# Gated window attention with a routed second stage on one core: each 1024 KB output store issued as four stores of one chunk

## The reference

```python
def xattn(x, cond):                       # 8 heads of 32 channels, a window of 16 columns
    q, k, v = pointwise(Wq, bq, x), pointwise(Wk, bk, cond), pointwise(Wv, bv, cond)
    k_win, v_win = windows(k), windows(v)
    attn = softmax(einsum('bhdt,bhdtw->bhtw', q, k_win) * 32 ** -0.5)
    return pointwise(Wo, bo, einsum('bhtw,bhdtw->bhdt', attn, v_win))

def ffn(h):                               # 64 experts, the top 8; a row is 2048 columns of one channel
    scores = softmax(h @ router_weight.T + router_bias)
    w_dense = the 8 largest of scores, zero elsewhere
    return h * w_dense.sum(-1) + w_dense @ expert_bias

x = x + tanh(g_xattn) * xattn(layernorm(x), ctx)
x = x + tanh(g_ffn) * ffn(layernorm(x))
```

## Time and profile before

| | |
|---|---|
| median of three runs | 1551.26 us (1549.26 to 1552.44) |
| the profiled execution: its own time | 1557.26 us |
| its span | 1555.1 us |
| busy, share of the span | TensorE 94%, VectorE 82%, ScalarE 74%, GpSimd 74% |
| mean granted TensorE clock | 0.972 of full |
| DMA | 365577 packets, 210.39 MB, mean 135 GB/s |
| written to HBM | 33.55 MB, in 32 stores |

### The profile page before, as it was taken

One profiled execution on the slowest core, in us unless ns is written; L12 is line 12 of the kernel. 1 busy time (PEld: TensorE's weight loads), 2 busy tenths in 40 slices (PEclk: granted clock), 3 DMA queues, 4 the chain that ended last, 5 costly groups with the idle time before them and its releaser, 6 DMA issues.

```text
span 1555.1 us, 66658 instructions
## 1 busy us (share of the span) xinstructions
PE 1464.6 (94%) x28162; PEld 1199.9 (77%) x28162; DVE 1276.5 (82%) x2970; ACT 1144.8 (74%) x2009; POOL 1148.0 (74%) x1110
## 2 busy tenths in 40 slices
PE   4799999999999999999999999999999999999985
PEld 3687887888787888878788788878888887778764
DVE  5578987888898887988888898888889888788764
ACT  4687877777787877788787877778787787767652
POOL 4688777787777877877787887778778777677661
PEclk8899999999999999999999999999999999899896
DMA  7455455445546554454555545455554545434132
GB/s 230 125 140 126 106 173 131 123 149 143 147 121 172 141 131 146 121 157 128 149 149 141 156 119 159 128 146 147 144 159 114 159 132 142 121 98 128 44 81 85
DMA packets 365577, 210.39 MB, mean 135 GB/s; under 512 B 294497, under 2 KB 295521, under 8 KB 361057
## 3 DMA queue, kind: packets, MB, share of 16 engines
q1 hardware_dynamic: 365280, 206.14, 49.1%
HBM read 136.88 MB, written 33.55 MB: 110 GB/s over the span
## 4 chain that ended last, share of the span: by engine, by line
PE 46%; DVE 35%; issue 8%; POOL 5%; ACT 3%; DMA 2%; SPq 1%; POOLq 0%; DVEq 0%; ACTq 0%
PE ps_j L1117 18%; PE ps_s L1177 7%; PE ps_a L1142 6%; PE ps_r L1219 5%; DVE prob_t L900 5%; PE ps_s L1117 3%; DVE p_sum L890 3%; DVE st_x L907 2%; DVE wq_lo L822 2%; POOL prob L493 2%; DVE lg L1046 2%; DVE st_in L804 2%; DVE v_turn L871 2%; PE ps_s L1172 2%; PE ps_a L1196 2%
## 5 line engine op out<-in xcount | busy, mean ns | idle before, releaser
L486 POOL TENSOR_TENSOR score<-score,p_inv 128x384 f32<-128x384 f32 x256 | 221.6, 866 | 119.5 <-DVE p_inv L894 117.0
L493 POOL TENSOR_TENSOR prob<-score,prob 128x384 f16<-128x384 f32 x256 | 266.0, 1039 | 38.8 <-ACT prob L644 38.3
L1177 PEld LDWEIGHTS ps_s<-kv_win,q_col 32*32 32x32 f32 x16384 | 198.0, 107 | 57.8 <-issue 57.8
L1177 PE MATMUL ps_s<-kv_win,q_col 32*32 32x48 f32 x16384 | 234.1, 205 | 2.4 <-issue 2.2
L900 DVE STREAM_TRANSPOSE prob_t<-prob 128x512 f32<-128x512 f32 x256 | 176.7, 699 | 55.1 <-POOL prob L493 54.9
L467 POOL TENSOR_TENSOR c_lo<-c_in,c_hi 128x1024 fp32r<-128x1024 f32 x64 | 152.7, 2386 | 89.5 <-ACT c_hi L618 89.5
L1142 PEld LDWEIGHTS ps_a<-prob_t,v_diag 128*128 128x128 f16 x6528 | 175.3, 98 | 50.1 <-DVE prob_t L900 32.6
L1142 PE MATMUL ps_a<-prob_t,v_diag 128*128 128x48 f16 (+2 forms) x6528 | 187.6, 183 | 26.2 <-DVE prob_t L900 19.4
L462 POOL TENSOR_TENSOR att_lo<-att,att_hi 128x512 fp32r<-128x512 f32 x128 | 161.8, 1275 | 51.5 <-ACT att_hi L604 50.3
L1117 PE MATMUL ps_j<-c_hi,wkv_hi 128*128 128x512 f32 x512 | 171.3, 416 | 19.6 <-DVE kv_win L864 10.6
L890 DVE TENSOR_REDUCE p_sum<-score 128x8 f32<-128x384 f32 x256 | 139.2, 544 | 54.3 <-ACT score L638 53.6
(11 more groups left out here) (149 smaller groups left out, 3318.0 us busy)
## 6 DMA issues: line engine op xcount, KB each, us to landing
v_diag<-v_turn SPq DMA_DIRECT2D x512, 68.0 KB, 2.8
c_in<-ctx_dram SPq DMA_DIRECT2D x64, 512.0 KB, 4.9
x_in<-x_dram SPq DMA_DIRECT2D x64, 512.0 KB, 5.5
x_res<-x_dram SPq DMA_DIRECT2D x64, 512.0 KB, 4.3
out_dram<-x SPq DMA_DIRECT2D x32, 1024.0 KB, 7.0
c_sq<-ctx_dram SPq DMA_DIRECT2D x60, 512.0 KB, 5.5
x<-ctx_dram SPq DMA_DIRECT2D x4, 512.0 KB, 6.1
x<-experts_dram SPq DMA_DIRECT2D x2, 512.0 KB, 10.6
```

The lines of the kernel that those rows point to most:

```text
L486: pool.tensor_tensor(score[:, u], score[:, u], p_inv[:, u, :].unsqueeze(2).to_broadcast([P, HALF, KEYS]), ALU.mult).then_inc(pm_rdy, 1)
L493: pool.tensor_tensor(part(prob[:, u % 2], 1)[:, :, 0:KEYS], score[:, u], part(prob[:, u % 2], 0)[:, :, 0:KEYS], ALU.subtract).then_inc(pl_ ...
L1177: ins = pe.matmul(s[head(h), n * KEYS:(n + 1) * KEYS], q_col[head(h), g, at:at + SUB], kv_win[c % 2][head(h), 0, g, at:at + KEYS], start=F ...
```

## The change

Each store of a group's 2048 columns becomes four stores of 512 columns. Each waits for the finish of its own chunk. The four are issued one behind another at the place where the single one stood. The totals on `out_st[g]` follow: 64 per batch and group in place of 16. Nothing else is touched.

```diff
                 if finishing(b, c):
 
                     g = c - 2
-                    rows_out = out[b - 1, g * P:(g + 1) * P, :]
-                    need(sp, fin_rdy, final(b - 1, g, NCH - 1))
-                    sp.dma_start(rows_out, x1[1 - par][:, g, :]).then_inc(out_st[g], 16)
+                    for j in range(NCH):
+                        rows_out = out[b - 1, g * P:(g + 1) * P, cols(j)]
+                        need(sp, fin_rdy, final(b - 1, g, j))
+                        sp.dma_start(rows_out, x1[1 - par][:, g, cols(j)]).then_inc(out_st[g], 16)
 
             walk(step)
             for g in range(G):
-                sp.wait_ge(out_st[g], 16 * (B + 1))
+                sp.wait_ge(out_st[g], 16 * NCH * B + 16)
...
                     if ch == 0:
 
-                        need(act, out_st[g], b * 16)
+                        need(act, out_st[g], (b - 1) * 16 * NCH + 16)
```

## The result

The changed kernel takes 1561.39 us in the median of 20 runs (1550.79 to 1569.28), the kernel before 1553.71 us in 20 runs beside them (1549.26 to 1559.47). The ratio is 1.0043, with a 95% interval from 1.0026 to 1.0060: 0.4% slower, where 0.1% less was forecast. The median of 1551.26 that the prediction started from was that of three runs, so 2.5 us of the distance between the 1549.6 us that it named and the 1561.39 us measured are its base. The profiled execution of the changed kernel took 1563.30 us, its span 1561.1 us, against 1557.26 and 1555.1.

The account below looks back on a forecast made before the run. TensorE and VectorE were taken to bound the kernel, with a store alone on the path only at the end. Middle cost 0 and tail gain 1.7 us took 1551.26 to 1549.6 us, range 1545.6 to 1552.6.

Parts of the forecast that it names:

- What bounds the kernel: Whole span: TensorE and VectorE make up 81% of the last-ending chain, DMA 2%; a store stands alone only at the end.
- The issues: SP's queue: 32 stores become 128 at 0.357 us each, 34 us more issuing, covered by SP's idle time.
- The tail: Last store after the last finish: only 256 KB remain, landing in 2.2 us instead of 3.9, gain 1.7 us.
- The middle: Finishing steps before the tail: added issues end 7.2 us before SP's next work and delay nothing, cost on the path 0.
- Rival B: TensorE's instruction loads come later, stalls grow and four clock falls at 3.0 us follow: 1561.6 us, chance 0.08.
- the point from which the clock falls: TensorE's stalls: each reaching the 1.25 us of the one at 575.15 may bring a fall of the granted clock.
- a stall by itself costs nothing: TensorE's stalls 8 to 9 us behind a batch's first store: 90.80 us with one, 90.72 without.
- the bound of the engine time: Output block with 2 KB packets: occupies each DMA engine at most 2.9 us instead of 2.55, 0.35 us longer.
- the engines are full either way: Argument against rival A: x_res and x_in precede the store, so the total ahead of the instruction packet stays.
- Rival A: TensorE's instruction loads wait for one 256 KB part only, removing a stall and clock fall: 3.0 us, 1546.6 us, chance 0.2.
- The rule against splitting: Batch transfers to at least 1 MiB, each having about 2.0 us constant share; four one after another would take 10.4 us.
- The edges: Upper end of the forecast range: 1551.3 us plus 1.2 us of spread between runs, given as 1552.6 us.

Follow-up runs that it names:

- e1: Kernel before with only the last batch's output blocks stored in four parts each, all others whole; ratio 0.9987, median 1549.40 us.
- e9: Kernel before with 64 small bf16 matrix products (128 instructions, half a block) added in the prologue; ratio 1.0119, median 1572.73 us.
- e4: Kernel before with two 512 KB stores of every second chunk (2 KB packets) behind the group's last finish; ratio 1.0010, median 1553.01 us.
- e2: The change's four chunk stores, but all issued behind the group's last finish; against the kernel before ratio 1.0010, median 1553.85 us.
- e11: Kernel before with two stores per group: chunks 0 to 2 behind the third finish, the last chunk behind the fourth; ratio 1.0021, median 1557.78 us.
- e5: The changed kernel run again, unaltered, beside other follow-up runs; against the kernel before ratio 1.0036, median 1560.41 us.
- e8: Kernel before with 64 float32 matrix products written in the prologue, which added 256 instructions, a whole block; ratio 1.0132, median 1575.49 us.
- e3: Kernel before with four 256 KB stores of 32 partitions and whole 8 KB rows, behind the last finish; ratio 1.0021, median 1553.45 us.
- e7: Kernel before with each group's store made four chunk stores and issued one step later, behind c_sq; ratio 1.0001, median 1554.43 us.

## Why the prediction was wrong

*What bounds the kernel*: right. No engine waits for out_dram after the change either, and SP's queue has 5.8 us to spare in the step shown.

*The issues*: the price was off, without effect. An issue takes 0.467 us at the median and not 0.357; four take 2.94 us in the step shown, so the fourth goes out over a microsecond later than the single store did, not 0.6. SP's waits for v_turn, which were to be shorter by 0.6 us in finishing steps, are 316.4 us in sum against 313.6.

*The tail*: right, 1.7 us forecast (1.1 to 1.8), 1.8 by SP's wait and 1.5 from the last finish to the end. e1, which has this part of the change alone, is some 2 us under the kernel before.

*The middle, "Cost on the path: 0"*: this is the step that failed; the runs show 7 to 8 us there. It was reasoned for SP and for those who wait for the kernel's own transfers, and there it holds. The instruction loads of TensorE were only taken up as rivals. They are the one user of the DMA engines that has no wait in the program: a transfer issued 0.6 us sooner, or held a little longer, meets them without a semaphore that shows it. Rival B had the mechanism, with a chance of 0.08, and 1561.6 us for it; measured were 1561.39. That it hits the number is chance in part: B had four more falls of the clock at 3.0 us. It also started from the base of 1551.26, so it had 10.3 us of loss where 7.7 were measured. The record shows two new falls, 6.9 us more at 1.2 GHz in all, and beside them batches that are longer without any, such as 294.63 to 387.41 with 92.78 us against 91.20. Nor is a stall of 1.25 us the point from which the clock falls: it fell behind one of 1.19 us (947.74) and not behind one of 1.44 (762.55).

*Why B was held to be unlikely*, in two steps. The first was that a stall by itself costs nothing, read from the batch of 90.80 us with one and that of 90.72 without. That was true of a stall of 0.9 us at that place. In e9, at another place, batches with a stall of about 0.9 us take 1.3 us longer. A cover was seen and not named, and so not measured. The second was the bound of the engine time, from 2 KB packets. Its size was right: 0.35 us per block, against 0.3 measured. Its cause was not: e4 has the same packets and none of the cost. The early issue was counted as harmless or useful, since "the engines are full either way". e2 against the change shows that it is the larger part of the loss.

*Rival A* falls. It held that the instruction packet would have to wait for one 256 KB part only. It came 8.0 us after x_in's issue instead of 7.6, behind the whole block as before. The rule on packet boundaries that it leaned on (the Trainium skill, "DMA: Bandwidth & Descriptors", section "Queues, rings and completion order") is not refuted by that, but neither the 2 KB packets of e4 nor the smaller stores of e2 brought the load forward by more than 0.2 us.

*The rule against splitting* (the Trainium skill, "DMA: Bandwidth & Descriptors", section "Bandwidth") warned rightly against the change, and for a reason that is not the one that decided. The fit that the prediction took from the Trainium skill ("DMA: Bandwidth & Descriptors", section "Anatomy of one DMA — SWDGE (gpsimd) path") is one for transfers that GpSimd issues; these go by SP. Here SP's landings overlap, four late stores a block cost the middle about 1 us in 1554 (e2), and the tail gained by being split.

*The edges*: 1551.3 and 1.2 make 1552.5, not 1552.6; nothing hangs on it.

*What stays open.* In which order an engine takes the instruction queue and queue 1, and so why an early issue puts the load further back, can't be read from these traces: a packet's record doesn't name its engine. e2 and e11 show that it is so, not how. What the last 3 us between e11 and the change are made of is open too.

*What the falls of the clock cost.* How many an execution has differs from run to run. The changed kernel's runs spread over 18.5 us and those of before over 10.2, and the profiled execution of e5 had the stalls of the change (13.3 us) and yet took 1550.65 us, the fastest of its twelve. Its clock over the middle (same columns as above; the third and the fourth of six stretches, all at 1.00):

```profile
600.00:800.00 200.00, 194.89 (x3893) 160.93 (x3882) 171.77 (x399) 155.42 (x274) 157.70 (x149) 1.00 0.55 145
800.00:1000.00 200.00, 195.81 (x3929) 161.47 (x3926) 175.07 (x423) 157.44 (x282) 156.57 (x150) 1.00 0.52 138
```

In the first profiled execution of the changed kernel the stretch from 800 to 1000 stands at 0.97. What stalls cost without a fall is read from twelve batches, from the first store to the first one of the thirteenth batch, in e1 and then in e5:

```profile
199.25 0.36 SPq L392 DMA_DIRECT2D out_dram<-x  x1
...
1292.00 0.36 SPq L392 DMA_DIRECT2D out_dram<-x  x1
```

```profile
201.58 2.80 SPq L391 DMA_DIRECT2D out_dram<-x  x4
...
1296.75 2.73 SPq L391 DMA_DIRECT2D out_dram<-x  x4
```

Both have no fall there. They take 1092.75 and 1095.17 us, with 5.9 and 12.7 us of stalls: 6.8 us more of stalls cost 2.4 us. The kernel before takes 1096.97 us for the same twelve (199.32 to 1296.29) with 10.2 us at 1.2 GHz, the changed one 1103.05 (200.01 to 1303.06) with 17.1. Without the falls they would be about where e1 and e5 are: an estimate from the prediction's 3.0 us for a fall of 6.8 us takes off 4.5 and 7.5 us and leaves 1092.5 and 1095.5.

All runs agree with that, since each has its mean granted clock on record. It is 0.9728 on average over the 20 of the changed kernel and 0.9734 in e5, and 0.9758 and 0.9759 over the runs of the kernel before beside e1 and e5. Within the 20 a lower clock goes with a longer time, 1.4 us for each 0.001 by a straight fit (correlation -0.87), which is also what one fall of 6.8 us in 1555 comes to. So of the 7 to 8 us lost in the middle some 3 to 4 go with the clock, some 2 with the stalls themselves, and 1 to 2 are not accounted for.

## What to carry to other kernels

Split the last store behind the last arithmetic, where nothing runs beside it, and leave the others whole; splitting all of them pays once and charges every time. Before a transfer is moved or made to start sooner, look for the instruction loads in the DMA record and for stalls of TensorE that nothing in the program explains: they wait behind the kernel's own transfers, and they cost according to what else stands at that place. A stall that costs nothing today is a place where half a microsecond more may not be free; and 128 added instructions of TensorE, which do nothing, cost 1.2% here by where they put the stalls.

## What the runs showed of the hardware that was not expected

- TensorE's instructions came in one packet of 0.02 MB at a time, and its work went on 2.3 to 3.0 us after the start of the packet that it stood still for (757.3 and 759.59 before, 760.1 and 762.55 after). While queue 1 was 96 to 99% busy, no such packet was moved for 3 us.
- All 107 stalls of 0.5 us and over stood at the same number modulo 256 of TensorE's records (193 or 194), in all fourteen kernels.
- A shift of the code by 256 instructions left the stalls where they were (e8), one by 128 moved them to the step behind the batch's second store (e9).
- After a stall of 1.61 us the granted clock stood at 0.50 until 861. After one of 1.44 us, at 762.55, the batch took 91.08 us, so a long stall does not bring a fall each time. In the fourteen profiled executions 37 stalls of 1.19 us and over stand between 190 and 1344 us. Behind 15 of them the clock fell within 2.4 us, for 3.4 or 6.8 us, behind 22 it did not, and there was no fall in that stretch without one.
- The time for which queue 1 occupied an engine was 763 us before and 761 to 766 in the other kernels with one store a block; 760 with two interleaved stores (e4), 766 and 767 with four late ones (e3, e2), 768 in e11, 771 with four deferred ones (e7), and 773 and 775 with the change. Packets of 2 KB alone did not lengthen it.
